# Decoder layer, cross-attention stage: late score tiles shifted in two parts around the closing scores, with the k product and the second norm's transposes between opening and closing

## What is computed

```python
x = layernorm(x + attn(x))       # linear attention with elu+1, then a feed-forward with a quantised gelu
x = layernorm(x + xattn(x, ctx)) # the stage that the change touches
x = layernorm(x + ffn(x))        # x @ W_shared.T + gate * (x @ W_expert.T) + bias
```

## Time and profile before

| quantity | value |
|---|---|
| median of 3 runs | 558.78 us (555.46 to 559.18) |
| the profiled execution: its own time | 559.04 us |
| the profiled execution: span from first to last instruction | 557.3 us |
| busy share: TensorE, VectorE, GpSimd, ScalarE | 89%, 73%, 67%, 65% |
| DMA: moved, mean rate | 17.38 MB, 31 GB/s |
| mean granted TensorE clock, as a share of 2.4 GHz | 0.984 |

### The profile page before, as it was taken

The page is one execution under the profiler, slowest core; times in us unless marked ns, Lnnn a source line. Parts: engine busy times, 40 slices in busy tenths (PEclk is TensorE's granted clock), DMA queues, the critical chain, the costliest instruction groups (busy, mean ns, idle before and its releaser), DMA issues. The chain is left out here.

```text
span 557.3 us, 22036 instructions
## 1 busy us (share of the span) xinstructions
PE 494.3 (89%) x8816; PEld 366.7 (66%) x8816; DVE 404.2 (73%) x1410; ACT 362.5 (65%) x681; POOL 371.7 (67%) x685
## 2 busy tenths in 40 slices
PE   2899999998999999997889999899998999999870
PEld 1777777775777767774566666667666666766660
DVE  1677777755777777647657888788888888888866
ACT  1566666656777777747756776577775776767641
POOL 6566666645577774733245878968788787988744
PEclk9999999999999999999989999899999999999987
DMA  6630000000000000001100201220111101110001
GB/s 167 171 116 2 3 2 1 4 2 1 2 0 3 1 1 1 2 2 40 31 22 4 44 19 43 49 50 26 29 50 51 51 21 32 51 50 23 23 2 57
DMA packets 24742, 17.38 MB, mean 31 GB/s; under 512 B 2112, under 2 KB 22464, under 8 KB 24640
## 3 DMA queue, kind: packets, MB, share of 16 engines
q1 hardware_dynamic: 24208, 15.90, 10.8%
q10 hardware_dynamic: 432, 0.07, 0.1%
HBM read 11.77 MB, written 4.19 MB: 29 GB/s over the span
## 5 line engine op out<-in xcount | busy, mean ns | idle before, releaser
L782 ACT ACTIVATE gel<-gel,row_scale 128x512 f32<-128x512 f32 x96 | 65.9, 720 | 20.1 <-DVE gel L1055 10.9
L789 ACT ACTIVATE gel<-pair 128x1024 f32<-128x1024 f32 x64 | 51.8, 809 | 32.0 <-PE pair L1415 31.2
L1042 DVE TENSOR_REDUCE neg_max<-pair 128x16 f32<-128x1024 f32 x64 | 60.4, 944 | 7.3 <-PE pair L1369 7.0
L1355 PEld LDWEIGHTS pair<-w,gel 128*128 128x128 f32 x512 | 60.4, 192 | 8.0 <-issue 5.7
L1355 PE MATMUL pair<-w,gel 128*128 128x128 f32 x512 | 62.3, 276 | 1.0 <-ACT gel L714 1.0
L1319 PE MATMUL pair<-hT,w 128*128 128x512 f32 x128 | 58.3, 596 | 1.3 <-ACT lev L709 1.3
L532 POOL TENSOR_SCALAR k_exp<-k_sb,quad_mask 128x512 f32<-128x512 f32 x64 | 43.0, 690 | 23.8 <-ACT k_sb L761 12.1
L1415 PE MATMUL pair<-ident,gel 128*128 128x128 f32 x384 | 56.0, 281 | 2.1 <-ACT gel L782 2.1
L1415 PEld LDWEIGHTS pair<-ident,gel 128*128 128x128 f32 x384 | 43.6, 142 | 19.1 <-issue 13.3
L1369 PE MATMUL pair<-k_exp,qT 32*32 32x128 f32 (+1 forms) x2048 | 45.2, 333 | 3.3 <-issue 3.2
L509 POOL TENSOR_TENSOR X<-X,proj_sb 128x512 f32<-128x512 f32 x16 | 20.3, 1270 | 35.6 <-ACT proj_sb L672 35.6
(11 more groups left out here) (140 smaller groups left out, 1227.1 us busy)
## 6 DMA issues: line engine op xcount, KB each, us to landing
X<-in_x SPq DMA_DIRECT2D x16, 256.0 KB, 3.2
cT<-in_ctx SPq DMA_DIRECT2D x16, 256.0 KB, 3.9
out_rows<-X SPq DMA_DIRECT2D x15, 256.0 KB, 2.4
mask_rows<-in_mask_early SPq DMA_DIRECT2D x16, 128.0 KB, 3.8
w<-in_L_attn_w SPq DMA_DIRECT2D x2, 256.0 KB, 3.5
out_rows<-X SPq DMA_DIRECT2D x2, 128.0 KB, 1.8
w_kv<-in_L_attn_wk SPq DMA_DIRECT2D x1, 64.0 KB, 3.2
w_q<-in_L_attn_wq ACTq DMA_DIRECT2D x1, 64.0 KB, 3.0
```

Of the source, the lines that this page charges most:

```text
L782: nc.scalar.activation(part, part, ACT.Exp, scale=row_scale[:, n:n + 1])\
L789: nc.scalar.activation(pT[par].rearrange("p (a c) -> p a c", a=2), turned, ACT.Copy)\
L1042: nc.vector.tensor_reduce(neg_max[par][:, :].rearrange("p (a h) -> p a h", a=2), scores, AX.X, ALU.max, negate=True).then_inc(max_ready, 1)
L1355: last = nc.tensor.matmul(bank(6 + q)[:, P * t:P * (t + 1)], gel[:, q, f, P * t:P * (t + 1)], w_2[:, f, :], start=(f == 0), stop=(f == NF ...
```

## The change

For late tiles `shift` becomes `shift_late(n, half)`, called twice. The first call waits only for the opening scores (`s_opened`) and takes the heads that are then complete, over both banks; the second takes the others behind the closing scores. Each is a maximum over 512 columns and one addition over 512 columns. `shift_early` is the old form for odd tiles. So that each half is complete by itself, the mask is now written per quad, with four products of half the width in the opening part and four in the closing part. `scores_close` also waits for the first half's `sub_ready`. TensorE's order changes: the k product stands between open and close in t = 0; the closing of the pair opened in t = 2 moves to t = 3, behind weigh and the second norm's transposes and ahead of the turn; `turn_y` goes from t = 3 to t = 0 (for g instead of s+2); `moe` of the fourth tile goes ahead of `turn_attended`; two of the three `moe` in t = 3 go ahead of weigh. `project_v` is cut into 16 products of 64 rows by 64 columns, whose result ScalarE copies with two instructions in place of four. On GpSimd the mixture goes ahead of `spread_v`. `gate_top` loses the copy of the first column (L1067). The banks of the four `moe` are permuted. The diff, cut to its core:

```diff
-MOE_BANK = [6, 4, 5, 5]
+MOE_BANK = [5, 6, 4, 5]
...
+                if exists(s - 2) and s < LAST:
+                    mixture(s - 2, p)
                 if exists(g):
                     spread_v(g, q)
                 if exists(s - 2) and s < LAST:
-                    mixture(s - 2, p)
                     last_norm(s - 2, p)
...
+                for h in range(2):
+                    rows = slice(h * S, (h + 1) * S)
+                    last = nc.scalar.activation(
+                        v2[q][rows, :, :, h, 0:DH],
+                        bank(first_bank(g, 5))[rows, :].rearrange("p (b i e) -> p b i e", i=HH, e=DH),
+                        ACT.Copy)
                 last.then_inc(v2_ready, 1)
...
+                    if t == TG - 1 and exists(prev):
+                        act.wait_ge(y2_xposed, prev + 1)
+                        after(act, moe_done, prev * TG)
+                        nc.scalar.activation(y2T[:, :], bank(6), ACT.Copy).then_inc(y2T_ready, 1)
+                    if t == TG - 1 and exists(nxt):
+                        probabilities(s * TG + t + 1, 0)
                     if exists(s):
                         copy_pT(s * TG + t, t % 2)
...
-                    if t == TG - 1 and exists(s + 2):
-                        copy_y(s + 2)
+                    if t == 0 and exists(nxt):
+                        copy_y(nxt)
...
-                        probabilities(s * TG + t + 1)
+                        probabilities(s * TG + t + 1, t % 2)
...
+                    if t == 0 and exists(s):
+                        probabilities(s * TG + 2, 0)
...
+            def shift_late(n, half):
+
+                dve.wait_ge(s_done if half or n == 0 else s_opened, n + 2 if n > 0 else n + 1)
+                part = slice(HQ * S * half, HQ * S * (half + 1))
+                scores = pair[0][:, :, part].rearrange("p a (h k) -> p a h k", k=S)
+                maxima = neg_max[0][:, :].rearrange("p (a j h) -> p a j h", a=2, j=2)[:, :, half, :]
+                nc.vector.tensor_reduce(maxima, scores, AX.X, ALU.max, negate=True)\
+                    .then_inc(max_ready, 1)
+                dve.wait_ge(max_ready, shifted(n, half))
+                after(dve, p_xposed, n - 1)
+                rows = probability_rows(n).rearrange("p (a j h k) -> p a j h k", a=2, j=2, k=S)
+                nc.vector.tensor_tensor(rows[:, :, half, :, :], scores,
+                                        maxima.unsqueeze(3).broadcast_to([P, 2, HQ, S]),
+                                        ALU.add).then_inc(sub_ready, 1)
+
+            def shift_early(n):
...
                 last.then_inc(top_ready, 1)
-                dve.wait_ge(top_ready, g * 2 + 1)
-                nc.vector.tensor_copy(top_z[:, :], top[:, :, 0]).then_inc(top_ready, 1)
-                dve.wait_ge(top_ready, g * 2 + 2)
-                nc.vector.tensor_tensor(top[:, :, :], top[:, :, :],
-                                        top_z[:, :].unsqueeze(2).broadcast_to([P, TG, TOPW]),
+                dve.wait_ge(top_ready, g + 1)
+                nc.vector.tensor_tensor(top_e[:, :, :], top[:, :, :],
+                                        top[:, :, 0].unsqueeze(2).broadcast_to([P, TG, TOPW]),
                                         ALU.subtract).then_inc(topd_ready, 1)
...
                         gate_top(old, p)
-                    if t == 0 and exists(s + 1):
-                        future_keys(s + 1, q)
+                    if exists(s) and t % 2 == 0 and n + 2 < NT:
+                        shift_late(n + 2, 0)
                     if t == 0 and exists(s):
                         after(dve, xatt_xposed, s - 1)
                         xattend(n, p, t)
+                    if t == 0 and exists(s + 1):
+                        future_keys(s + 1, q)
                     if t == 1 and exists(s):
-                        shift(n + 1, 0)
+                        shift_late(n + 1, 1)
                     if t == 1 and exists(prev):
                         residual(prev, 6, range(TG))
                     if t == 1 and exists(s):
-                        shift(n + 2, 1)
+                        shift_early(n + 2)
                         xattend(n, p, t)
                     if t == 1 and exists(old):
                         gate_weights(old)
                     if t == 2 and exists(s):
                         xattend(n, p, t)
+                    if n == -1:
+                        shift_late(0, 0)
                     if t == 3 and exists(s + 1):
-                        shift(n + 1, 0)
+                        shift_late(n + 1, 1)
...
+                        shift_early(n + 2)
...
+            def quad_scores(*parts):
+
+                for n, quads in parts:
+                    width = QW if n % 2 else S
+                    for quad in quads:
+                        rows = slice(quad * QW, (quad + 1) * QW)
+                        heads = slice(quad % 2 * HQ * width, (quad % 2 + 1) * HQ * width)
+                        future = causal_bf[rows, :].rearrange("p (h k) -> p h k", k=S)
+                        nc.tensor.matmul(pair[n % 2][:, quad // 2, heads],
+                                         quad_ident[rows, :, :].rearrange("p b q -> p (b q)"),
+                                         future[:, 0:HQ, S - width:], start=True, stop=False)
...
-                for n in ns:
-                    quad_scores(n, (0, 2) if n % 2 else (1, 3)).then_inc(s_done, 1)
+                if len(ns) > 1:
+                    pe.wait_ge(sub_ready, shifted(ns[0], 0))
+                quad_scores(*((n, (0, 2) if n % 2 else (1, 3)) for n in ns)).then_inc(s_done, len(ns))
...
+                for u in range(2 * TG):
+                    for h in range(2):
+                        last = nc.tensor.matmul(bank(first_bank(g, 5))[h * S:(h + 1) * S,
+                                                                       FH * u:FH * (u + 1)],
+                                                cT[q][:, S * u:S * (u + 1)],
+                                                w_xv[:, FH * h:FH * (h + 1)],
+                                                start=True, stop=True)
                 last.then_inc(xv_done, 1)
...
+                    if t == 3 and exists(r):
+                        pe.wait_ge(ln_b.done, r + 1)
+                        transposes(y2, bank(6), y2_xposed)
+                    if t == 3 and exists(s) and exists(g):
+                        scores_close(n + 1, n + 2)
                     if exists(s):
                         turn_probabilities(n, t)
-                    if n == 0:
-                        turn_y(1)
+                    if t == 0 and exists(s - 2):
+                        pe.wait_ge(moe_ready, (s - 2) * TG + 1)
+                        moe(s - 2, TG - 1)
                     if t == 0 and exists(r):
                         pe.wait_ge(xatt_ready, r * TG + TG)
-                        after(pe, moe_ready, (s - 1) * TG - 3)
+                        after(pe, moe_ready, (s - 1) * TG - 2)
                         turn_attended(q, 6, range(TG))
-                    if t == 0 and exists(s - 2):
-                        pe.wait_ge(moe_ready, (s - 2) * TG + 3)
-                        moe(s - 2, TG - 1)
+                    if t == 0 and exists(g):
+                        after(pe, moe_ready, (s - 1) * TG - 1)
+                        after(pe, q_ready, g)
+                        turn_y(g)
...
-                        after(pe, moe_ready, (s - 1) * TG - 2)
...
-                    if t == 3 and exists(s + 2):
-                        pe.wait_ge(q_ready, g + 1)
-                        turn_y(s + 2)
...
-                    if t == 3 and exists(r):
-                        pe.wait_ge(ln_b.done, r + 1)
-                        transposes(y2, bank(6), y2_xposed)
                     if exists(s) and t % 2 == 0 and n + 2 < NT:
                         scores_open(n + 2, n + 3)
+                    if t == 3 and exists(r) and s < LAST:
+                        pe.wait_ge(y2T_ready, r + 1)
+                        if exists(g):
+                            pe.wait_ge(v2_ready, g + 1)
+                        for u in range(2):
+                            moe(r, u)
...
-                    if exists(s) and t % 2 == 0 and n + 2 < NT:
-                        scores_close(n + 2, n + 3)
...
                         project_qk(cT[q], w_xk, bank(5), xk_done)
+                    if exists(s) and t == 0:
+                        scores_close(n + 2, n + 3)
                     if t == 3 and exists(r) and s < LAST:
-                        pe.wait_ge(y2T_ready, r + 1)
-                        for u in range(TG - 1):
-                            if u == 1 and exists(g):
-                                pe.wait_ge(yT_ready, min(s + 3, NG))
-                            if u == 2 and exists(g):
-                                pe.wait_ge(v2_ready, g + 1)
-                            moe(r, u)
+                        if exists(g):
```

(43 more changed lines are left out.)

77 lines of the change are left out of this document (23 added, 54 removed).

## The result

The changed kernel takes 564.06 us against 558.22 for the kernel before: ratio 1.0122, 95% interval 1.008 to 1.0164. It is slower, by 1.2%; 562.0 was predicted, in a range of 554 to 569. One execution of each, and one of e8, was far slower (952.41, 586.52 and 794.85 us); the ratios leave these out, and without them the medians are 562.73, 557.67 and, for e8, 551.56. The profiled execution took 562.31 us with a span of 560.6.

The account below looks back on a forecast made before the run. It took a 17.23 us loop through VectorE and GpSimd as the bound. A new round of 9.19 + 8.31 = 17.50 adds 3.6 us over thirteen rounds, less 0.4 at the end: 562.0 us predicted, range 554 to 569.

Parts of the forecast that it names:

- within 1%: Whole kernel: measured time within 1% of the kernel before; chance 0.53.
- slower by over 1%: Whole kernel: the masks' 0.22 and a fifth of the forecast's 0.45, together chance 0.31.
- the sign of being right: Cross-attention rounds: a length of 17.3 to 17.7 us would show the prediction right.
- the "slower" rival: Opening and closing parts: masks cost by product, not column, 0.16 more each; round 17.93, total 567; chance 0.22.
- the 1.9 us to spare: GpSimd after the change: mixture ends 7.56 us behind the residual, VectorE needs some 9.4 to the last statistics.
- the two loops through GpSimd: Kernel before: the predicted one runs residual, second norm, `spread_v`, mixture, last statistics, late shift, 17.23 us; its twin starts from `last_norm`.
- The loop named for after: New round: VectorE and TensorE alternate through two closing parts, 9.19 + 8.31 = 17.50 us against 17.22.
- first half-round: From the close of t = 0 to that of t = 3: VectorE's way, 9.19 us.
- the term with the two prices: Each opening or closing part on TensorE: 0.75 us if columns set the masks' time, 0.91 if a mask costs the same whatever its width.
- The other price: TensorE's four masks per part at 0.32 us whatever their width, making each part 0.91; kept for the range.
- the half shift until TensorE goes on: VectorE's first half of a late shift until TensorE continues: 1.49 us, in both half-rounds.
- - 0.4: End of the kernel: two `gate_top` copies leave the last group's chain, 0.4 us less.

Follow-up runs that it names:

- e8: Kernel before with GpSimd's mixture moved ahead of `spread_v` and `gate_top` without its copy: 552.04 us, ratio 0.9881.
- e1: Kernel before with one edit, GpSimd's mixture moved ahead of `spread_v`: 552.71 us, ratio 0.9924.
- e2: Changed kernel with GpSimd's mixture put back behind `spread_v`: 562.49 us, ratio 1.0099 to the kernel before.
- e4: Changed kernel with VectorE's gate weights moved behind the late shift's first part and the division of t = 2: 561.62 us, ratio 1.0083.
- e10: Changed kernel with the v product in four and its copy in four instructions, as before: 562.06 us, ratio 1.0084.
- e9: Changed kernel with the second norm's transposes and their copy, in the last round alone, back behind turn and half output product: 562.03 us, ratio 1.0076.
- e6: Changed kernel with the second norm's transposes and their copy back behind the turn: 612.12 us, ratio 1.0964.
- e7: Changed kernel with the k product behind the closing scores of t = 0: 576.66 us, ratio 1.0312.
- e3: Changed kernel with both parts of a late shift behind the closing scores, and closing waiting for no shift: 597.69 us, ratio 1.0725.
- e5: Changed kernel without the four mask products of the closing part, a time only: 558.07 us, ratio 1.0024.

## Why the prediction was right, and where its numbers were off

The time lies in the range and 2.1 us from the number forecast, but not in the case that was given the most weight: "within 1%" had 0.53 and "slower by over 1%" 0.31, and 1.2% was measured, with an interval on both sides of 1%. The round of 17.86 lies outside the 17.3 to 17.7 named as the sign of being right, and beyond the 17.65 at which the "slower" rival was to decide.

That GpSimd's mixture bound the kernel before is confirmed from both sides: moving it alone gives 16.97 a round (e1), and restoring its order in the changed kernel costs nothing (e2), as the 1.9 us to spare said. Which of the two loops through GpSimd one names makes no difference to the change, since both hold `spread_v`; the prediction saw one of them.

The loop named for after is the right one. Its first half-round is 392.56 - 383.18 = 9.38 (9.19 predicted), bound by VectorE (e4). Its second is 17.86 - 9.38 = 8.48; here the prediction had 8.31 for VectorE and 8.26 for TensorE and took the larger. It is TensorE's way: opening passes to weigh at 399.17, and VectorE's next half starts 0.31 later, at 399.48. That is the distance behind both closing parts too (383.99 to 384.30, 393.37 to 393.68), and `gate_top` by itself would have let it start some 0.1 earlier, at 398.87 + 0.47 = 399.34. e4 leaves this half-round at 8.47.

The step that was mis-sized is the part of masks and scores, the term with the two prices. The prediction took 0.75, which is 0.16 for the narrow masks; four of them take 0.21 and the part is 0.81. It stands once in the first half-round and twice, as closing and as opening, in TensorE's way through the second: 0.18 in all, about half of the 0.36 by which the round was too short. The other price, 0.32 for the masks, was wrong too. Next comes the half shift until TensorE goes on, 391.00 to 392.56 = 1.56 (1.49 taken), also on both ways. The gate weights took 1.30 (1.25), the y transposes 0.53 (0.44), turn and third `moe` 0.05 more each. Some terms were shorter: the weighing 0.68 (0.76), the fourth `moe` 0.44 (0.49), the start of VectorE behind the scores 0.31 (0.34). None is large. The distances were read from the timeline of another order, and here their sum came out low. The Trainium skill's formula for a load (TensorE: Matmul & The Clock Gate, section LDWEIGHTS) gives 107 ns for 128 columns and so, as an estimate, 0.43 for four masks; the trace has 0.21.

Off the loop, `project_v` took up to 1.15 where 0.93 was taken, and the wait ahead of the opening that follows was 0.21 for ScalarE's copy in place of 0.6 for VectorE. Both are hidden: e10 leaves the round as it is.

At the end the prediction had - 0.4 and overlooked a move: in the last round the norm's transposes go ahead of the half output product for which VectorE waits, which costs 1.4 (e9). From the last k product to the end it is 2.6 more than before; the other 1.2 stay open.

Two costs were set to nothing and were nothing in the round: the v product with its copy (e10), and TensorE's wait of 0.7 for the second norm, which VectorE covers in the first half-round. Of the latter only 0.3 can be had by making VectorE faster: in e4 the closing follows the transposes directly.

Of the total, 0.64 x 14 rounds would be 9.0 us, and 2.6 at the end. The medians differ by 5.8 (5.1 by the second pair in the section on the result) and the profiled executions by 3.3. In these the 14 rounds took 508.13 - 257.65 = 250.5 against 507.47 - 258.41 = 249.1, so only 1.4 of the 9.0 is left. The difference lies in disturbed rounds. The profiled execution of before has three with a wait of over 1 us that nothing releases ("issue"), two of them with a fall of the clock, and they are 20.44, 20.45 and 18.41 us long. The changed one has four waits that nothing releases too, of 0.71 to 1.26, but no fall of the clock between its first and last k product and no round above 18.32. One of those of before:

```profile
357.97 0.40 PE L1369 MATMUL pair<-k_exp,qT 32*32 32x128 f32 x2 [1.49 <-issue]
```

```profile
357.00:360.00 3.00, 2.03 (x10) 1.83 (x11) 1.55 (x2) 0.55 (x1) 2.71 (x5) 0.71 0.02 5
```

So the mechanism was right, but that 562.0 came so near is in part luck: a round too short by 0.36 and an end too short by 3.0, against disturbances of before that the prediction counted as if they stayed. What these waits are stays open, and so does why the changed kernel loses less by them.

## What to carry to other kernels

When an engine seems full, close the loop in numbers before touching its order: here one moved call on GpSimd gave 0.8% (e1), and the whole rewrite of TensorE's and VectorE's orders, which holds the same move, ends some 2% behind it. And look for a second loop of the same length before trusting the first. Splitting an operation so that a consumer can start early adds a hand-over in each direction; with two such hand-overs in a round, every short piece between them (masks, latencies of 0.3) is on the path. Where two ways to a point are within 0.1 us, add up both to the end, and check the last round by itself.

## What the runs showed of the hardware beyond this

Waits of TensorE of 1.36 to 1.76 us were mostly followed by stretches at 1.2 GHz: those of 1.49 and 1.71 in the kernel before, and ten of the eleven in e6. That made the 1.4 us that e6 adds to an undisturbed round into some 3.4 in all: (550.76 - 293.75) / 12 = 21.4 from k product to k product, against (508.13 - 292.06) / 12 = 18.0 in the changed kernel. The waits of up to 0.7 us in each round of the changed kernel and the ones of 1.05 to 1.12 in each round of e7 left the mean granted clock at 0.98 to 0.99.

The length of one wait doesn't settle it, though. The clock fell with one of 0.99 in e4 (granted clock 0.60 from 445.5 to 448.5). It fell behind some of e3's waits of 1.13 and not behind others, nor behind its two of 1.48 and 1.49. A longer one, in e5, was followed by no fall; the granted clock is 1.00 from 355 to 364:

```profile
355.59 0.43 PE L1452 MATMUL pair<-v,gel 128*32 128x18 f32 x28 [2.14 <-issue]
```

What settles it isn't shown.

The 64-row halves of the v product, 32 records of 64 columns, stand between 388.03 and 389.39 less a wait of 0.21, so within 1.15 us. One after another they would need 1.86, an estimate: twice the 0.93 that the prediction read for 8 records of 128 columns. They run at least largely side by side.
